# A graph layer on one Trainium2 core: edge hits and the GELU rows placed in PSUM banks instead of SBUF

## The reference, cut to what matters

```python
xn = _layernorm(x)                                    # x: 3125 nodes x 256
x = x + _L0_gnn_ref(xn, src, dst, edge_type_8, ...) + _L0_mix_ref(xn[None], ...)[0]
x = x + _L0_ffn_ref(_layernorm(x)[None], ...)[0]      # 32 experts, each node takes one

def _L0_gnn_ref(node_feats, src, dst, edge_types, ...):   # 50000 edges, 8 relations, 4 bases
    W = jnp.einsum('rb,bio->rio', comp, basis)
    msgs = jnp.einsum('ni,rio->nro', node_feats, W)[src, edge_types]
    agg = jax.ops.segment_sum(msgs, dst, num_segments=node_feats.shape[0])
    h = jax.nn.gelu(agg + node_feats @ loop_w + h_bias + node_feats, approximate=False)
    mu = jnp.mean(h, -1); var = jnp.mean(jnp.square(h - mu), -1)
    return (h - mu) * jax.lax.rsqrt(var + LN_EPS) * ln_gamma + ln_beta
```

## Time and profile before

| | us |
|---|---|
| median of 3 runs (lowest to highest) | 623.22 (621.47 to 623.65) |
| the profiled execution: its time | 624.2 |
| the profiled execution: its span | 622.3 |

### The profile page before, as it was taken

The page is one execution under the profiler, slowest core; times in us unless marked ns, Lnnn a source line. Parts: engine busy times, 40 slices in busy tenths (PEclk is TensorE's granted clock), DMA queues, the critical chain, the costliest instruction groups (busy, mean ns, idle before and its releaser), DMA issues.

```text
span 622.3 us, 10665 instructions
## 1 busy us (share of the span) xinstructions
PE 522.4 (84%) x3112; PEld 442.2 (71%) x3112; DVE 394.6 (63%) x1468; ACT 215.1 (35%) x437; POOL 433.6 (70%) x448
## 2 busy tenths in 40 slices
PE   0666989998767999999999999999998882389990
PEld 0566889997657777888887878787877761277880
DVE  6899677776544645767666666756665326626882
ACT  6685633321107112424334342424241001155430
POOL 7777777777777777777777777777777730474662
PEclk9978999999988699999999999999995556599995
DMA  8994333333354334445454544444444328473221
GB/s 275 268 261 130 97 108 103 102 102 97 104 163 136 103 102 127 144 141 155 129 153 132 154 141 145 143 141 143 141 140 121 107 60 248 132 208 117 79 85 40
DMA packets 41362, 85.24 MB, mean 137 GB/s; under 512 B 10793, under 2 KB 23018, under 8 KB 41107
## 3 DMA queue, kind: packets, MB, share of 16 engines
q0 software_dynamic: 21920, 60.90, 34.0%
q1 hardware_dynamic: 18372, 22.95, 11.8%
q10 hardware_dynamic: 1008, 0.65, 0.3%
HBM read 71.66 MB, written 12.81 MB: 136 GB/s over the span
## 4 chain that ended last, share of the span: by engine, by line
POOL 34%; PE 29%; issue 13%; DMA 10%; DVE 10%; ACT 1%; DVEq 0%; ACTq 0%; POOLq 0%
POOL gath L592 20%; PE ps L939 11%; POOL acc_raw L592 11%; DMA gath<-xn_d,src_i 7%; PE ps L1010 6%; PE ps L1213 4%; PE ps L1204 3%; POOL both L638 3%; PE ps L993 2%; DVE raw_stats L1321 1%; DMA rel_of<-in_relation_of 1%; DMA acc_raw<-xn_d,src_i 1%; DVE stats L1295 1%; DVE acc_raw L1415 1%; PE ps L1033 1%
## 5 line engine op out<-in xcount | busy, mean ns | idle before, releaser
L592 POOL DMA_INDIRECT gath<-xn_d,src_i x263 | 255.0, 970 | 80.2 <-issue 72.6
L939 PEld LDWEIGHTS ps<-wmat,gath 128*128 128x128 f32 x1052 | 155.5, 214 | 45.6 <-issue 21.0
L939 PE MATMUL ps<-wmat,gath 128*128 128x80 f32 (+1 forms) x1052 | 167.1, 307 | 17.9 <-DMA gath<-xn_d,src_i 16.6
L1390 DVE TENSOR_TENSOR wmat<-hit,wts 128x576 f32<-128x576 f32 (+1 forms) x100 | 63.1, 631 | 108.8 <-PE ps L939 107.5
L592 POOL DMA_INDIRECT acc_raw<-xn_d,src_i x96 | 95.7, 997 | 29.3 <-issue 24.4
L1415 DVE TENSOR_TENSOR acc_raw<-acc_raw,ps 128x144 f32 (+1 forms) x392 | 88.6, 267 | 40.2 <-PE ps L939 33.7
L939 PE MATMUL ps<-wmat,acc_raw 128*128 128x144 f32 x512 | 71.4, 292 | 14.1 <-ACT acc_raw L700 7.9
L939 PEld LDWEIGHTS ps<-wmat,acc_raw 128*128 128x128 f32 x512 | 67.9, 193 | 18.6 <-issue 11.0
L1010 PE MATMUL ps<-wk_et,acc_raw 128*128 128x256 f32 (+1 forms) x200 | 53.6, 393 | 0.9 <-DVE acc_raw L1415 0.9
L796 ACT ACTIVATE both<-both,eps_col 128x1 f32<-128x1 f32 (+1 forms) x25 | 7.4, 294 | 134.1 <-DVE both L1480 134.1
L1010 PE MATMUL ps<-wq_wv,acc_raw 128*128 128x256 f32 (+1 forms) x200 | 51.9, 383 | 0.0
(11 more groups left out here) (233 smaller groups left out, 732.5 us busy)
## 6 DMA issues: line engine op xcount, KB each, us to landing
rows_d<-both SPq DMA_DIRECT2D x24, 256.0 KB, 2.3
gath<-xn_d,src_i POOLq DMA_INDIRECT x263, 2.8
both<-in_x SPq DMA_DIRECT2D x24, 128.0 KB, 3.5
both<-in_x SPq DMA_DIRECT2D x4, 640.0 KB, 9.7
xn_d<-both SPq DMA_DIRECT2D x4, 640.0 KB
acc_raw<-in_w_t SPq DMA_DIRECT2D x1, 2080.0 KB
acc_raw<-in_w_t SPq DMA_DIRECT2D x1, 2048.0 KB, 7.2
acc_raw<-xn_d,src_i POOLq DMA_INDIRECT x96, 2.8
```

The source lines that it names most:

```text
L592: g.indirect_dma_start(place_of(n), None, table, bass.IndirectOffsetOnAxis(ap=src_i[:, n:n + 1], axis=0)).then_inc(done, 16)
L939: ins = t_.matmul(ps_edge[quarter][:, m * w:(m + 1) * w], place_of(n)[:, m * P:(m + 1) * P], wmat_tiles[:, k, 0:w], start=k == pair[0], st ...
L1390: d.tensor_tensor(made, hit[:, :, 0:width(q)].unsqueeze(2).to_broadcast([P, w, B, width(q)]), wts[:, :, cut].rearrange("p b t -> p t b").u ...
```

## The change

The table `hit` is no longer an SBUF buffer. `build_hit` and `build_weights` are one function: for half h of an octet the table is written into columns 368 and up of the bank ps0 (h = 0) or ps2 (h = 1), whose first 288 columns take the quarter's products, and is read from there. Since the bank must not be in PE's use, the table is built after the wait on `multiplied`, directly ahead of the multiplication that reads it.

`h` and `y` are gone as SBUF buffers too: GELU is written back over the first 256 columns of the bank `mix(t)`, `y` over it again, and `second_stats` reads it there. So the bank of a tile is in use until the `second_stats` of the tile have read it, and `early(t)` waits on `var_b` of tile t-2 in place of `gelu_done` and `y_made`. GELU's own wait on `y_made` goes.

```diff
-                if t >= 2:
-                    act.wait_ge(c.y_made, t - 1)
-                s.activation(h[0:n, t % 2, :], mix(t)[0:n, 0:D], ACT.Gelu).then_inc(c.gelu_done, 1)
+                s.activation(mix(t)[0:n, 0:D], mix(t)[0:n, 0:D], ACT.Gelu).then_inc(c.gelu_done, 1)
...
                 if t >= 2:
-                    pe.wait_ge(c.gelu_done, t - 1)
-                    pe.wait_ge(c.y_made, t - 1)
+                    pe.wait_ge(c.var_b, t - 1)
...
+            def build_weights(q, half):
...
+                if n > 0:
+                    v.wait_ge(wmat_built, n)
+                if q > 0:
+                    v.wait_ge(multiplied, OCT * q + half * w + w)
+                hit = ps_edge[2 * half][:, HIT_AT:HIT_AT + w * width(q)].rearrange("p (k w) -> p k w", w=width(q))
+                d.tensor_tensor(hit, rel[:, cut].unsqueeze(2)..., iota[:, 0:width(q)]..., ALU.is_equal).then_inc(hit_built, 1)
                 v.wait_ge(hit_built, n + 1)
-                d.tensor_tensor(made, hit[:, :, 0:width(q)].unsqueeze(2)..., wts[...]..., ALU.mult).then_inc(wmat_built, 1)
+                d.tensor_tensor(made, hit.unsqueeze(2)..., wts[...]..., ALU.mult).then_inc(wmat_built, 1)
...
                     if w % 2 == 0:
                         build_weights(q + 1, half)
-                if OCT * (q + 1 + half) < ETAB:
-                    build_hit(q + 1 + half, 1 - half)
...
-                at = c.own.mark(d.bn_stats(stat_a[0:n, :], h[0:n, t % 2, :]))
+                at = c.own.mark(d.bn_stats(stat_a[0:n, :], mix(t)[0:n, 0:D]))
...
-                d.scalar_tensor_tensor(y[0:n, :], h[0:n, t % 2, :], mv_a[0:n, 0:1], gam_bc[0:n, :], ALU.subtract, ALU.mult).then_inc(c.y_made, 1)
+                d.scalar_tensor_tensor(mix(t)[0:n, 0:D], mix(t)[0:n, 0:D], mv_a[0:n, 0:1], gam_bc[0:n, :], ALU.subtract, ALU.mult).then_inc(c.y_made, 1)
...
-                at = c.own.mark(d.scalar_tensor_tensor(x2, y[0:n, :], rs_a[0:n, :], x2, ALU.mult, ALU.add))
+                at = c.own.mark(d.scalar_tensor_tensor(x2, mix(t)[0:n, 0:D], rs_a[0:n, :], x2, ALU.mult, ALU.add))
```

More of the change, by code:

```diff
@@ L31 @@
 WIN, SLIM = 36, 20
+HIT_AT = 512 - 4 * WIN
 NARROW = 26
@@ L77 @@
 assert TS * TG == P and TS * TW == TC * P and HIGH * P + 4 * D <= NPAD and EARLY * OCT % STAGE == 0
-assert OCT == 4 * PAIR and ETAB % ROWG == 0 and NT % GROUPS == 0 and PAIRS % 2 == 0
+assert KD * 4 * WIN <= HIT_AT and OCT == 4 * PAIR and ETAB % ROWG == 0 and NT % GROUPS == 0 and PAIRS % 2 == 0
 assert len(STEP) == INLINE and STARTS[-1] + 3 < NOCT and SOFT0 + CHUNKS == EARLY
@@ L159, in gps_layer @@
         wmat = sb("wmat", [P, OCT, B, WIN])
-        hit = sb("hit", [P, OCT // 2, WIN])
+        hit_slow = sb("hit_slow", [P, P])
         wmat_tiles = wmat[:, :, :, :].rearrange("p k b w -> p k (b w)")
@@ L246, in gps_layer @@
         xr = xn_raw[:, 14 * D:17 * D].rearrange("p (j f) -> p j f", j=3)
-        h = xn_raw[:, 17 * D:19 * D].rearrange("p (j f) -> p j f", j=2)
-        y = xn_raw[:, 19 * D:20 * D]
         x2nt = xn_raw[:, 20 * D:22 * D].rearrange("p (j k n) -> p j k n", j=2, k=KD)
@@ L1371, in _ @@
             v.sem_inc(added, 4 * KD)
[L1373 to L1380, removed]
             def build_weights(q, half):
@@ L1384, in build_weights @@
                 n = 2 * q + half
-                cut = ds(OCT * q + half * w, w) if not isinstance(q, int) else slice(OCT * q + half * w, OCT * q + half * w + w)
-                if not isinstance(q, int) or q > 0:
+                cut = slice(OCT * q + half * w, OCT * q + half * w + w)
+                if n > 0:
+                    v.wait_ge(wmat_built, n)
+                if q > 0:
                     v.wait_ge(multiplied, OCT * q + half * w + w)
+                hit = ps_edge[2 * half][:, HIT_AT:HIT_AT + w * width(q)].rearrange("p (k w) -> p k w", w=width(q))
+                d.tensor_tensor(hit, rel[:, cut].unsqueeze(2).to_broadcast([P, w, width(q)]),
+                                iota[:, 0:width(q)].unsqueeze(1).to_broadcast([P, w, width(q)]), ALU.is_equal).then_inc(hit_built, 1)
                 v.wait_ge(hit_built, n + 1)
                 made = wmat_tiles[:, half * w:half * w + w, 0:B * width(q)].rearrange("p k (b w) -> p k b w", b=B)
-                d.tensor_tensor(made, hit[:, :, 0:width(q)].unsqueeze(2).to_broadcast([P, w, B, width(q)]),
+                d.tensor_tensor(made, hit.unsqueeze(2).to_broadcast([P, w, B, width(q)]),
                                 wts[:, :, cut].rearrange("p b t -> p t b").unsqueeze(3).to_broadcast([P, w, B, width(q)]),
@@ L1394, in _ @@
             for half in range(2):
-                build_hit(0, half)
                 build_weights(0, half)
-            build_hit(1, 0)
             def add_identity():
@@ L1757, in _ @@
             far_dst = cols[:, 5:6]
-            sgath = hit[:, :, :].rearrange("p a w -> p (a w)")[:, 0:P]
+            sgath = hit_slow[:, :]
             with v.If(redo > 0):
```

## The result

| | before | after |
|---|---|---|
| median, us (lowest to highest, 20 runs each) | 623.39 (621.47 to 626.8) | 626.45 (623.45 to 631.18) |
| ratio, 95% interval | | 1.0049 (1.0028 to 1.0070) |
| the profiled execution: time, span | 624.2, 622.3 | 629.0, 627.2 |

The forecast was 3 us faster, 620.2, and the result lies 0.45 us outside its range.

The account below looks back on a forecast made before the run. POOL's back-to-back gathers were taken as the bound, PE a close second. -5.25 us up to tile 0, +6.7 from tile 2 to 24 and -4.45 behind that made -3.0 us: 623.2 to 620.2 us, range 614.5 to 626.

Parts of the forecast that it names:

- up to tile 0: Path to tile 0's start: 5.5 us of long gathers taken away, 0.25 us added by the table's order, -5.25 us.
- test 1: POOL's gathers: none under the weights' multiplication longer than 1.0 us, groups of line 592 with means near 950 ns.
- test 2: PE's `early`: starts every 10.3 us in narrow octets, some 11.1 in wide, its idle time put down to DVE's variance.
- test 3: Between tiles 2 and 24, gathers wait for PE's edges more than 0.3 us.
- Rival D: POOL's gathers not freed, held up by DVE's other SBUF traffic, PE held up all the same: 626.3 us, chance 0.13.
- Rival C: PSUM operands slow on DVE, 0.07 us more per instruction, 0.2 us in each of 23 stalls: some 624.8, chance 0.2.
- B: POOL stays the bound, `var_b` sooner or PE makes the stall good, only 10.3 us count: 612.9, chance 0.12.
- PE's clock: PE's half-clock spells may fall elsewhere; one of 5 us costs or gives some 2 us, chance 0.05.
- Part 4: PE's `early` waits on `var_b`: stall of 0.51 us per narrow octet, 0.94 in wide ones, 13.6 us together.
- part 2: On DVE, the table now ahead of the weights: +0.12 us per half octet, +0.25 us ahead of tile 0.
- The last stretch: Tile 24 to last gather's end: POOL at its 8 places' limit, 31 gathers, 38.8 us for 43.25, -4.45 us.
- rival A: The forecast itself: POOL freed, PE held up, 0.1 us error per stall: 617.5 to 622.8, half of the chance.

Follow-up runs that it names:

- e0: The kernel after, unchanged, run a second time beside the kernel before; 626.70 us, ratio 1.0007.
- e2: Kernel before with GELU's rows and `y` in the PSUM bank and the wait on `var_b`, table still in SBUF; 626.93 us, ratio 1.0063.
- e6: Kernel before with `early` waiting on `var_b` in place of `gelu_done` and `y_made`, no buffer moved; 627.25 us, ratio 1.0057.
- e3: Kernel after with `y` alone back in SBUF and `early` waiting on `y_made`; 616.62 us, ratio 0.9868.
- e4: Kernel after with `early` waiting on the instruction that reads the bank last, not on the variance; 614.24 us, ratio 0.9874.
- e7: Kernel after with the second norm's statistics taken twice, the second time behind a wait for the first; 636.23 us, ratio 1.0173.
- e8: Kernel after with e4's wait on the last reader and e7's doubled statistics; 616.68 us, ratio 0.9861.
- e9: e4 run a second time, unchanged, on another chip; 614.22 us, ratio 0.9845 of the kernel before.
- e1: Kernel after with `h`, `y` and the waits as before, so only the table is in PSUM; 616.96 us, ratio 0.9887.
- e5: Kernel before with the table, still in SBUF, built directly ahead of the weights; 624.09 us, ratio 0.9998.

## Why the prediction was wrong

By its own steps, against the profiled executions of after and e0:

| stretch | forecast | after | e0 |
|---|---|---|---|
| up to tile 0 | -5.25 | -2.45 | -2.06 |
| tile 0 to 24 | +6.7 | +8.52 | +8.54 |
| tile 24 to the end of the last gather | -4.45 | -3.72 | -3.73 |
| behind it | 0 | +2.5 | +1.3 |
| sum | -3.0 | +4.9 | +4.1 |

**The mechanism was right.** The gathers were freed (test 1), PE became the bound and waits for the variance (test 2), gathers wait for PE, up to 1.3 us between the tiles (test 3). Rival D falls by the groups' means, though its 626.3 us is what was measured: there the number fits and the mechanism doesn't. Rival C falls: the weights' multiplication took 757 and 491 ns (758 and 492 before), the multiply and add of the row 484 (486). B falls by the period. What failed are sizes in the sum: the stall, which was too small, and PE's clock, which the sum put at nothing.

**Part 4, the stall, mis-sized: 0.51 us was 0.60**, and this is the step of the mechanism that failed. The larger part of the miss in the profile, 5.3 of 7.9 us, stands ahead of tile 0 and behind the last gather, where the sum had put PE's clock at nothing. The race was read rightly as 0.36 us, and e2 and e6 confirm it with 10.23 us. The 0.12 of part 2 was too small: I took the pair's row from the start of the kernel, where the table's instruction is released by nothing on PE. Behind a wait for PE it costs 0.06 more at its start, and 0.20 in all, in PSUM and in SBUF alike. The wide octets took 10.86 to 11.25 us where some 11.1 were foreseen. 0.09 us more, 23 times, make 2.1 us, and 1.8 is what tile 0 to 24 missed by. I had put the whole stall behind tile 2; tile 2's own, 0.9 us, lies ahead of it (235.88 - 215.64 = 20.24 against 19.32).

**The last stretch, -3.7 for -4.45:** with PE slower than POOL, POOL was at the limit of its places, as said, but gather 360 starts 0.33 us behind tile 24 and gather 362 waits 0.74 us more for PE; 39.53 us for 38.8.

**Up to tile 0, -2.4 for -5.25.** What POOL gains here is as forecast: gather 160 starts at 205.21 us in after and 205.12 in e0, where it started at 211.38. What comes late is tile 0 itself. e3, e4, e7, e8 and e9 have the code of after up to tile 0, and start it at 212.17, 210.86, 211.93, 212.02 and 213.20, as the forecast of 212.8 wanted. What differs is PE's clock. Windows from 160 to 216 us (busy us of PE, PEld, DVE, ACT, POOL with their counts, granted clock, DMA share, GB/s), after, then e4:

```profile
160.00:216.00 56.00, 47.56 (x244) 42.15 (x243) 32.59 (x111) 15.71 (x24) 40.98 (x44) 0.76 0.42 127
```

```profile
160.00:216.00 56.00, 43.86 (x260) 37.02 (x259) 33.34 (x114) 15.32 (x24) 42.41 (x45) 0.94 0.44 130
```

At 0.76, PE stood at the lower of its two levels (1.2 of 2.4 GHz) for some 27 of these 56 us (2 x 0.24 x 56), was busy for longer with fewer products, and held the gathers up; in e4, for some 7 us, and there PE waits 6.8 us for gathers in the same window (after: 1.7). The start of tile 0 follows the low clock right ahead of it. The granted clock from 195 us to the start of tile 0 in all profiles, and the time at the lower level by the same sum:

| | kernels with short gathers | | | | | | | | with long gathers | | | |
|---|---|---|---|---|---|---|---|---|---|---|---|---|
| run | e4 | e1 | e3 | e7 | e8 | e9 | after | e0 | e2 | e5 | before | e6 |
| clock | 1.00 | 0.90 | 0.90 | 0.90 | 0.90 | 0.81 | 0.67 | 0.68 | 1.00 | 0.92 | 0.78 | 0.80 |
| us at the lower level | 0 | 3.4 | 3.4 | 3.4 | 3.4 | 6.9 | 13.6 | 13.5 | 0 | 3.6 | 10.2 | 10.3 |
| start of tile 0 | 210.86 | 211.99 | 212.17 | 211.93 | 212.02 | 213.20 | 215.64 | 216.03 | 215.62 | 217.53 | 218.09 | 220.77 |

At like clock the short gathers bring tile 0 forward by 4.8 us (e4 against e2) or 5.5 (e1 against e5), which bears the -5.25 out, and each microsecond at the lower level goes with some 0.35. The prediction gave such spells 0.05 of the chance and "some 2 us" for one of 5 us; 13.6 us of them cost 4.8. Both profiles of after have the long spell and none of its five variants has, so whether chance alone gives it to them stays open.

**Behind the last gather, +2.5 and +1.3 for 0.** All kernels have nearly the same code there. The eleven others take from 117.1 to 123.3 us and after takes 119.6, with no order by kernel, and the profile of before has the shortest of all. So the term looks like the chance of single executions; no run was made to show it.

**What turned the sign.** The stall and the last stretch alone take the -3.0 to -0.5 us, still no gain to measure. The late tile 0 and the tail put the rest on top, +5.4 in the first profile. By the medians, +3.1 and +2.3, it is some 3.6 and 2.8 on the average of the runs; where the runs that were not profiled lose it is not shown. The sum was a small difference of two large terms, as its last sentence says, with a range that stopped just short of the outcome in which all the errors point one way. Rival C's price of some 0.2 us in each stall, with its mechanism, was wrong. A stall longer by 0.09 us, as it came, lies within the 0.1 us of error that rival A allows; with it and the last stretch alone the result would have stayed inside A. It is the late tile 0, 2.8 us where A allows 1, and the tail, where it allows nothing, that carry it out. Nor did the text look at what the new wait names: line 1476, the last reader of `y`, stood in the path it added up, 0.7 us ahead of the variance. That one wait is worth 12 us by the medians and 8.8 to 11.2 between tile 0 and the end of the last gather.

## What to carry to other kernels

When a buffer's release is tied to a semaphore, name its last reader, not a signal that happens to exist a few instructions later: here 0.68 us of statistics between the two cost PE some 0.6 us in each of 23 tiles, and all of the gain. Where two engines are within 2% of each other, freeing one is worth only what the other has in hand, so a stall that was partly hidden (e6 costs 4 us by the medians, 0.5 between tile 0 and the last gather) is paid in full (12 us, 8.8 to 11.2) once the bound is gone. And price a reordered pair of instructions in the place where it will stand, behind the wait that will release it.

## What the runs showed of the hardware

- A gather on POOL is held up while DVE's weights' multiplication runs with two SBUF inputs: 1.33 us with the table in SBUF, 0.94 in PSUM, for the same instruction and nearly the same overlap.
- DVE reads PSUM no slower than SBUF here (757 and 758 ns, 484 and 486). Writing the table into PSUM costs 7 to 10 ns: 318 and 251 ns, against 308 and 244 for e5's table in SBUF in the same order. In its old place, behind the adds, it took 302 and 237.
- Two dependent DVE instructions start 0.28 us apart for 0.25 us of the first; two independent ones overlapped, 0.15 for 0.23.
- The granted clock of PE from 160 to 216 us was 0.76 in one profile and 0.94 in another, with the same code up to tile 0, which started 4.8 us later in the first. Over eight profiles each microsecond at the lower level between 195 us and tile 0 goes with some 0.35 us (an estimate from the table above).
